# Query and key operands of an attention stage: a scratch tensor laid out by head group, gathered by six transfers instead of sixteen

## What is computed

```python
def poincare_fully_connected(x, z, r, c):
    lam = 2.0 / (1.0 - c * jnp.sum(x * x, axis=-1, keepdims=True))
    z_norm = jnp.maximum(jnp.linalg.norm(z, axis=0), EPS)
    two_cr = 2.0 * c_sqrt * r
    inner = x @ (z / z_norm)
    v = 2.0 * z_norm / c_sqrt * jnp.arcsinh(c_sqrt * lam * inner * jnp.cosh(two_cr) - (lam - 1.0) * jnp.sinh(two_cr))
    w = jnp.sinh(c_sqrt * v) / c_sqrt
    return w / (1.0 + jnp.sqrt(1.0 + c * jnp.sum(w * w, axis=-1, keepdims=True)))

Q = poincare_fully_connected(x, z_q, b_q, C)
K = poincare_fully_connected(x, z_k, b_k, C)
V = x @ w_v.T + b_v
scores = jnp.einsum('bhqd,bhkd->bhqk', Qh, Kh) / np.sqrt(D_K)
probs = jax.nn.softmax(scores, axis=-1)
out = jnp.einsum('bhqk,bhkd->bhqd', probs, Vh)
```

## Time and profile before

| | us |
|---|---|
| median of 3 runs | 3177.55 |
| profiled execution, own time | 3171.44 |
| its span | 3169.6 |
| TensorE matmul busy | 2838.4 (90%) |
| ScalarE busy | 2026.5 (64%) |
| VectorE busy | 1846.0 (58%) |
| GpSimd busy | 1273.0 (40%) |
| gather transfers (`b_st<-b_scratch`) | 512 of 128.0 KB, median 7.0 us to landing |
| parts stores (`b_scratch<-b_parts`) | 32 of 768.0 KB, median 7.7 us to landing |

### The profile page before, as it was taken

One profiled execution on the slowest core, in us unless ns is written; L12 is line 12 of the kernel. 1 busy time (PEld: TensorE's weight loads), 2 busy tenths in 40 slices (PEclk: granted clock), 3 DMA queues, 4 the chain that ended last, 5 costly groups with the idle time before them and its releaser, 6 DMA issues. The chain is left out here.

```text
span 3169.6 us, 38539 instructions
## 1 busy us (share of the span) xinstructions
PE 2838.4 (90%) x12161; PEld 1226.5 (39%) x12161; DVE 1846.0 (58%) x2420; ACT 2026.5 (64%) x2650; POOL 1273.0 (40%) x786
## 2 busy tenths in 40 slices
PE   3899999999979999657999999999999999969997
PEld 1455555555554444322323232323233332234443
DVE  8899999999973453454443444444444441144444
ACT  6454555455425555325889797978878889835554
POOL 4798899889861220141314131322313230021210
PEclk7899999999999999778999999999999999989999
DMA  2010001010012211206263635535553627231112
GB/s 80 1 37 27 30 26 36 23 33 26 24 56 75 80 53 53 67 11 132 29 146 42 134 54 94 93 73 92 92 94 58 116 46 128 27 114 48 60 53 67
DMA packets 163998, 200.30 MB, mean 63 GB/s; under 512 B 16504, under 2 KB 118272, under 8 KB 163840
## 3 DMA queue, kind: packets, MB, share of 16 engines
q1 hardware_dynamic: 163840, 198.25, 28.4%
HBM read 139.49 MB, written 58.72 MB: 63 GB/s over the span
## 5 line engine op out<-in xcount | busy, mean ns | idle before, releaser
L1859 ACT ACTIVATE b_pr<-b_ps 128x1024 f32<-128x1024 f32 x1024 | 1002.8, 1025 | 255.5 <-PE b_ps L1956 251.2
L1956 PE MATMUL b_ps<-b_st 128*128 128x512 bf16 x2048 | 591.2, 386 | 71.0 <-DMA b_st<-b_scratch 31.6
L1938 PE MATMUL b_acc<-b_pr,b_vaug 128*32 128x512 f32 x4096 | 549.0, 608 | 0.4 <-ACT b_pr L1859 0.4
L1956 PEld LDWEIGHTS b_ps<-b_st 128*128 128x128 bf16 x2048 | 150.3, 98 | 649.5 <-ACT b_pr L1859 381.9
L1257 PE MATMUL f_po<-f_s,f_w 128*128 128x512 f32 x768 | 355.0, 605 | 9.4 <-DVE f_xr L1042 5.9
L1030 DVE TENSOR_TENSOR f_turned<-f_cs,f_s 128x1024 f32<-128x1024 f32 x96 | 119.3, 1243 | 364.4 <-ACT f_cs L1159 359.4
L635 PE MATMUL a_pv<-a_xnT,a_wv 128*128 128x512 f32 x512 | 251.2, 614 | 52.8 <-DVE a_mem L403 38.7
L1123 ACT ACTIVATE f_h<-f_po,f_b 128x512 f32<-128x512 f32 x192 | 131.9, 687 | 218.1 <-PE f_po L1257 218.1
L627 PE MATMUL a_pu<-a_xnT,a_wk 128*128 128x512 f32 x512 | 238.3, 609 | 29.2 <-DVE a_frac L355 23.2
L1575 POOL TENSOR_TENSOR b_SQ<-b_A 128x1024 f32<-128x1024 f32 x32 | 64.7, 2021 | 467.1 <-DVE b_A L1672 467.1
L674 PE MATMUL a_py<-a_wo,a_out 128*128 128x256 f32 x960 | 229.1, 382 | 0.0
(11 more groups left out here) (259 smaller groups left out, 4694.4 us busy)
## 6 DMA issues: line engine op xcount, KB each, us to landing
b_st<-b_scratch SPq DMA_DIRECT2D x512, 128.0 KB, 7.0
b_scratch<-b_parts SPq DMA_DIRECT2D x32, 768.0 KB, 7.7
f_xl<-x SPq DMA_DIRECT2D x16, 1024.0 KB, 5.5
f_xr<-x SPq DMA_DIRECT2D x16, 1024.0 KB, 6.8
a_xl<-in_L_attn_a_x_dram SPq DMA_DIRECT2D x16, 512.0 KB, 4.2
x<-a_xr SPq DMA_DIRECT2D x32, 256.0 KB, 2.2
x<-f_xr SPq DMA_DIRECT2D x8, 1024.0 KB, 4.5
b_xl<-x SPq DMA_DIRECT2D x8, 1024.0 KB, 7.8
```

The lines of the kernel that those rows point to most:

```text
L1859: nc.scalar.activation(pr[:, 4 * (blk % 2) + j, :], ps[:, j % 2, :], ACT.Exp, scale=SC).then_inc(S["probs_done"], 1)
L1938: x = nc.tensor.matmul(acc[32 * j:32 * j + 32, h * 512:(h + 1) * 512], vaug[:, kt, c:c + 32], pr[:, 4 * (kt % 2) + j, h * 512:(h + 1) * 51 ...
L1956: x = nc.tensor.matmul(ps[:, j % 2, h * 512:(h + 1) * 512], st[:, g % 2, 1, j, kt * P:(kt + 1) * P], st[:, g % 2, 0, j, h * 512:(h + 1) * ...
```

## The change

The scratch tensor gets the order part, head group, feature in head, head in group, row, so that the four heads' rows for one feature stand behind one another, 8 KB. For the store to stay one of 128 partitions, the columns of the weights are permuted once, by a ScalarE copy into a new tile `zp`, from (group, head, feature) to (group, feature, head), and the biases are loaded in that order, by eight transfers of 64 values in place of four of 128. A gather is now six transfers: of the 8 runs of 16 partitions of Q the first three hold part 0, the next three part 1, the last two part 2, and each of these is one transfer that reads its 16 rows three times (or twice) by a leading dimension of step 0; for K parts 0 to 2, 0 to 2, and 0 to 1 are one transfer each. Bytes moved to SBUF by a gather are the same, 2 MB.

```diff
-Q_PART = [0, 0, 0, 1, 1, 1, 2, 2]
-K_PART = [0, 1, 2, 0, 1, 2, 0, 1]
+Q_RUNS = [(0, 3, 0), (3, 3, 1), (6, 2, 2)]
+K_RUNS = [(0, 3, 0), (3, 3, 0), (6, 2, 0)]
...
-    scratch = nc.dram_tensor("b_scratch", [2, 3, D, T], BF16, kind="Internal").ap()
+    scratch = nc.dram_tensor("b_scratch", [2, 3, H // 4, DK, 4, T], BF16, kind="Internal").ap()
...
+        zp = s.sb("zp", [P, 2, KD, D])
...
-        N_W = 16 * 8
-        N_G = 16 * 16
+        N_W = 16 * 12
+        N_G = 16 * (len(Q_RUNS) + len(K_RUNS))
...
-                sp.dma_start(scratch[o, :, f * P:(f + 1) * P].rearrange("w p t -> p w t"), parts[:, o, :, f, :])\
+                sp.dma_start(scratch[o, :, 2 * f:2 * f + 2].rearrange("w g d j t -> (g d j) w t"), parts[:, o, :, f, :])\
                     .then_inc(parts_stored[f], 16)
...
-            for o, part in enumerate((Q_PART, K_PART)):
-                for i, w in enumerate(part):
-                    sp.dma_start(st[i * DK:(i + 1) * DK, slot, o],
-                                 scratch[o, w, 64 * g:64 * g + 64, :].rearrange("(h d) t -> d h t", d=DK))\
-                        .then_inc(st_loaded[slot], 16)
+            for i, n, w in Q_RUNS:
+                sp.dma_start(st[i * DK:(i + n) * DK, slot, 0].rearrange("p h t -> p (h t)"),
+                             scratch[0, w, g].rearrange("d h t -> d (h t)").unsqueeze(0).broadcast_to([n, DK, 4 * T]))\
+                    .then_inc(st_loaded[slot], 16)
+            for i, n, w in K_RUNS:
+                sp.dma_start(st[i * DK:(i + n) * DK, slot, 1].rearrange("p h t -> p (h t)"),
+                             scratch[1, w:w + n, g].rearrange("w d h t -> w d (h t)")).then_inc(st_loaded[slot], 16)
...
-                    for f in range(KD):
-                        sp.dma_start(rcol[:, 2 * o + f:2 * o + f + 1],
-                                     r[f * P:(f + 1) * P].rearrange("(p o) -> p o", o=1)).then_inc(S["w_loaded"], 16)
+                    for g in range(G):
+                        c = 2 * o + g // 2
+                        sp.dma_start(rcol[g % 2 * 64:g % 2 * 64 + 64, c:c + 1],
+                                     r[64 * g:64 * g + 64].rearrange("(j d) -> d j", d=DK),
+                                     allow_slow_non_contiguous=True).then_inc(S["w_loaded"], 16)
...
                 dve.wait_ge(S["w_loaded"], N_W)
-                nc.vector.tensor_tensor(A[:, 0, :], z_sb[:].rearrange("p o k n -> p (o k n)"),
-                                        z_sb[:].rearrange("p o k n -> p (o k n)"), ALU.mult).then_inc(S["setup_v"], 1)
+                dve.wait_ge(S["z_done"], 1)
+                nc.vector.tensor_tensor(A[:, 0, :], zp[:].rearrange("p o k n -> p (o k n)"),
+                                        zp[:].rearrange("p o k n -> p (o k n)"), ALU.mult).then_inc(S["setup_v"], 1)
...
                 act.wait_ge(S["w_loaded"], N_W)
+                nc.scalar.activation(zp[:].rearrange("p o k (g d j) -> p (o k g) d j", g=G, d=DK),
+                                     z_sb[:].rearrange("p o k (g j d) -> p (o k g) d j", g=G, d=DK), ACT.Copy).then_inc(S["z_done"], 1)
...
-                            x = nc.tensor.matmul(bank, z_sb[:, q // 2, k, (q % 2) * P:(q % 2 + 1) * P], xnT[:, k, c],
+                            x = nc.tensor.matmul(bank, zp[:, q // 2, k, (q % 2) * P:(q % 2 + 1) * P], xnT[:, k, c],
```

More of the change, by code:

```diff
@@ L1424, in phase_b @@
         zn2, zn2m = cols[:, 3, :], cols[:, 4, :]
-        names = ("w_loaded setup_p setup_v setup_a setup_m xl_loaded xr_loaded stored stats_done mv_done rstd_done "
+        names = ("w_loaded z_done setup_p setup_v setup_a setup_m xl_loaded xr_loaded stored stats_done mv_done rstd_done "
                  "xn_done lam_done dlam_done misc_ready misc_taken inT_done a_done sq_done root_done abs_done y_done ln_done e_done "
```

## The result

The changed kernel takes 3323.71 us (median of 4 runs, 3319.01 to 3327.42) where the kernel before takes 3176.46 (4 runs): a ratio of 1.0463, 95% interval 1.0445 to 1.0482. Predicted were 3320 us. The profiled execution took 3319.01, 147.6 us more than the profiled one before.

What follows compares the result with a forecast made beforehand. TensorE was taken to bound the attention blocks, with the gather hidden except at the start. Later batch starts, batch 7's late groups, clock and setup summed to 142.6 us, giving 3320 us; range 3260 to 3430.

Steps and rivals of the forecast that it cites:

- D: New gather's time from first issue to landing: 34.5 us, of which 31.5 bytes and 3.0 issue and landing; bounds 31.6 to 38.0.
- starts of the eight batches: TensorE's first scores of each batch begin later because the gather takes longer: 116.8 us in all.
- batch 7, group 1: Gather of group 1 in the last batch, which has no work for a next batch: 8.8 us late.
- batch 7, group 2: Gather of group 2 in the last batch, behind the output's store and one load: 6.7 us late.
- batch 7, group 3: Gather of group 3 in the last batch: 0.5 us late.
- setup: Four more bias loads and the copy of `z` delay the norms: 1.3 us, bounds 0 and 4.
- clock: TensorE's lower clock after five new stalls, 1.7 us lost at each: 8.5 us.
- Groups 1 of batches 1 to 6: Gathers of group 1 in these batches, due 35.6 us after issue: in time with 1.1 us to spare.
- At nothing: Items priced at no cost or gain: 320 fewer issues on SyncE, the store, products from `zp` instead of `z`.
- the 2.1 us of group 2: Groups 2 and 3 of batches 1 to 5: gather done in 42.3 us of a 44.4 us group, hidden by 2.1.
- A: Rival: the gather's transfers run on all 16 engines, gaining only in batch 0: -7.1 us, 3170.4 us; chance 14%.
- B: Rival: same few engines, slower still, group 1 late in every batch once the gather passes 35.6 us: 3509 us; chance 8%.

Runs made afterwards that it cites:

- e1: Changed kernel with only its gather back to sixteen transfers of 16 partitions, outer dimension 16 on both sides: 3181.64 us, 1.0025 of the kernel before.
- e2: Kernel before, old layout and 2 KB runs, only its gather leading with 3 or 2, in 24 transfers: 3321.41 and 3321.02 us.
- e3_wide16: Changed kernel with another permutation and choice of parts, gather in eight transfers of 48, 32 or 16 rows on both sides: 3157.87 us, 0.9954 of the kernel before.

## Why the prediction was right

**What bounds.** Stage b is a chain that a late gather lengthens one for one; this held. From its first load to its last store the stage took 1454.8 us before and 1606.1 after, 151.3 more. The stages behind it were 3.4 us shorter in this one execution, with nothing in them changed, so that the whole, 147.6, came nearer to the 142.6 predicted than the stage did, and that is chance.

**How a transfer is dealt out.** From 8 rows on 8 engines and 16 on 16 I took the common divisor of 48 and 3. The 16 small packets of a gather show it, and e1 and e2 show that it alone matters. The Trainium skill ("DMA: Bandwidth & Descriptors", "Why a DMA increments its semaphore by 16 and not by 1") has the rule for the number and says that the lowest-numbered engines are taken. The packet counts agree with the number in every shape tried here (3 and 2 engines for 48 against 3 and 32 against 2, 16 for 48 against 48); which engines they are no view shows, only that the six transfers share them.

**The gather's length.** D was 35.1 to 36.1 us against 34.5. If the rate is the 25 GB/s that three engines at 75 show, the fixed part is about 4 and not 3.0 us; the bounds of 31.6 and 38.0 held it.

**The terms.**

| term | predicted | measured |
|---|---|---|
| starts of the eight batches | 116.8 | 125.1 |
| batch 7, group 1 | 8.8 | 9.5 |
| batch 7, group 2 | 6.7 | 4.2 |
| batch 7, group 3 | 0.5 | none |
| setup | 1.3 | 3.1 |
| clock | 8.5 | 11.3 |
| what is left | | -1.9 |
| sum, stage b | 142.6 | 151.3 |

The starts are mis-sized by D's 0.6 to 1.6 us, eight times. Groups 1 of batches 1 to 6, forecast 1.1 us in time, were in time, although D itself had eaten most of that. The clock was mis-sized too. The prediction took one loop return, that into batch 2, for all: 0.66 granted for 5 us, 1.7 us lost. Behind the return into batch 3 TensorE ran wholly at the lower level, in the kernel before already; the start of batch 1 in the changed kernel is more like the return into batch 2:

```profile
1954.30:1959.30 5.00, 5.00 (x16) 1.06 (x16) 0.69 (x1) 2.18 (x3) 0.00 (x0) 0.50 0.01 3
...
1653.00:1658.00 5.00, 4.80 (x23) 1.10 (x24) 0.69 (x1) 2.78 (x3) 0.00 (x0) 0.68 0.04 17
```

Summed as for e3_wide16, over 20 us behind each place, the missing clock is 11.0 us before (batch 0 and the loop's four) and 22.4 us in the changed kernel: 12.4 at the same five places and 10.0 at the five new ones, 1.4 to 3.1 each. So the term is 11.3 and not 8.5. That a missing microsecond of clock costs one of time is taken, as in the prediction, and the 1.9 us by which the terms exceed the stage are not traced.

The setup was, for its size, the worst of the terms. Its rows, the counterpart of the earlier trace rows:

```profile
1322.12 2.78 SPq L1479 DMA_DIRECT2D b_cols<-in_L_attn_b_b_q_dram  x4
...
1333.10 1.93 ACT L1826 ACTIVATE b_zp<-b_z 128x1024 f32<-128x1024 f32 x1 [26.63 <-DMA b_bvb<-in_L_attn_b_b_v_dram]
...
1340.15 0.16 DVE L1791 COPY b_cols<-b_pm 128x4 f32<-128x4 f32 x1 [3.73 <-PE b_pm L1988]
```

The copy took 1.93 us, near my upper bound for it and not the 1.1 in the sum, the issue of the bias loads 3.1 us more and not 2.5, and the norms arrived at 1340.15, where GpSimd's rows of x no longer covered them. The stage's first gather was issued 113.5 us after its first load, 110.5 before: 3.1 us.

**At nothing.** The fewer issues on SyncE show no gain in any term; the queue even became a worse place. The output's store, which stands behind the slow gather, held the load behind it for 185.5 us in seven batches (before, it was 85.1):

```profile
SPq L1505 <- DMA x<-b_xr: 185.5, 7, 31.8
```

It stayed hidden, as the 2.1 us of group 2 had promised. I had not seen that the issue itself would be held, 13 us a time; in batch 0 it delayed the issue of the gather of group 1 to 1452.53, and the 43 us of work in group 0 (1469.69 to 1512.85, where the gather of group 2 is let go) hid that.

**The rivals.** A (all engines) fell with the packet counts. Its price is tested by e3_wide16: in batch 0 a wide gather gave 3.8 us and not 8.4, since 48, 32 and 16 partitions do not take 400 GB/s, and elsewhere it gave what I had put at nothing, the shorter returns. Where all 16 engines do work, as in e3_wide16, the gain is 15 us and not the 7.1 of A, and clear of noise: A's price was too small, and most of the gain lay where A had none. B did not come: D passed 35.6 in some batches, but only by half a microsecond, and no group 1 but that of batch 7 waited.

## What to carry to other kernels

Look at the slowest dimension of both sides of each DMA: in every shape tried here it set how many engines move the data, and a leading 3 or a repeat of step 0 confines 384 KB to three of them. Fewer, longer transfers are no gain by themselves; lay the scratch tensor out so that all outer dimensions merge into one of 16, 32 or 48 rows (a permutation of features, and another choice of which part meets which, were enough here). And keep large transfers that nobody waits for away from the return of a hardware loop.

## What the runs showed of the hardware that I had not expected

- A loop's return stopped TensorE for 2.1 to 2.5 us when the DMA engines were idle and for 3.1 to 4.8 when a store kept them full. Moving one store was worth 0.44%.
- The rate of a row of transfers on all 16 engines rose with the partitions of SBUF that each one writes or reads: 125 to 158 GB/s with 16 partitions, 131 to 262, mean 190, with 48, 32 and 16 mixed, 371 to 410 with 128 (the stores, which run the other way). Three engines gave 74 to 82, with runs of 2 KB as of 8 KB.
- SyncE was held at an issue behind a gather on three engines: 7 to 15 us for two transfers that took 0.9 to 2.3 us in the kernel before.
